# Keys and values of the second attention, projected during routing and kept in device memory

## What is computed

```python
qp = q @ Wq.T
kv = latent_kv @ Wkv_expand.T        # latent_kv is the context: (4, 256, 64)
k, v = jnp.split(kv, 2, axis=-1)
...                                  # 16 heads of 16
scores = jnp.einsum('bhqd,bhkd->bhqk', qh, kh) * inv_sqrt_d
scores = jnp.where(causal, scores, jnp.finfo(scores.dtype).min)
attn = jax.nn.softmax(scores, axis=-1)
out = jnp.einsum('bhqk,bhkd->bhqd', attn, vh)
```

## Time and profile before

| what | value |
|---|---|
| median of 3 runs | 613.92 us (612.71 to 614.38) |
| the profiled execution: its time, its span | 607.06 us, 605.3 us |
| PE busy | 425.7 us (70%), 2738 matmuls |
| DVE busy | 346.5 us (57%) |
| ACT busy | 184.0 us (30%) |
| POOL busy | 146.3 us (24%) |
| mean granted clock of PE | 0.834 of full |

### The profile page before, as it was taken

The page is one execution under the profiler, slowest core; times in us unless marked ns, Lnnn a source line. Parts: engine busy times, 40 slices in busy tenths (PEclk is TensorE's granted clock), DMA queues, the critical chain, the costliest instruction groups (busy, mean ns, idle before and its releaser), DMA issues.

```text
span 605.3 us, 9222 instructions
## 1 busy us (share of the span) xinstructions
PE 425.7 (70%) x2738; PEld 355.7 (59%) x2738; DVE 346.5 (57%) x1050; ACT 184.0 (30%) x377; POOL 146.3 (24%) x154
## 2 busy tenths in 40 slices
PE   5065553302999999997136637899699978999686
PEld 3043342202998889885025425787488856887586
DVE  2978875396344444443367803487547883681554
ACT  3212210100333333343611412525252342517231
POOL 1306675673000000002775370001710000000000
PEclk9976565555999999997557756999779996999899
DMA  7996222266699999993332130000310000000000
GB/s 272 427 410 264 88 96 79 78 238 211 209 301 322 324 312 326 377 396 128 100 91 67 38 104 0 1 2 16 100 44 0 2 0 0 18 2 2 2 17 18
DMA packets 36693, 82.96 MB, mean 137 GB/s; under 512 B 6000, under 2 KB 16048, under 8 KB 34864
## 3 DMA queue, kind: packets, MB, share of 16 engines
q1 hardware_dynamic: 22800, 55.83, 26.3%
q0 software_dynamic: 6144, 16.79, 8.6%
q10 hardware_dynamic: 7712, 9.90, 4.6%
HBM read 50.44 MB, written 31.92 MB: 136 GB/s over the span
## 4 chain that ended last, share of the span: by engine, by line
PE 52%; DVE 15%; issue 12%; ACT 7%; POOL 6%; another core or an unknown queue 4%; DMA 2%; SPq 1%; DVEq 0%; POOLq 0%; ACTq 0%
PE PS L555 11%; PE PS L565 7%; POOL slots_in L432 5%; PE PS L644 4%; PE PS L618 4%; PE PS L542 3%; PE PS L764 2%; PE PS L657 2%; PE PS L712 2%; PE PS L659 2%; PE PS L658 2%; DVE TH L1312 2%; DVE WORK L1049 2%; DVE TOP L1045 2%
## 5 line engine op out<-in xcount | busy, mean ns | idle before, releaser
L442 POOL DMA_INDIRECT GB<-slots_out,IDXG x64 | 68.4, 1069 | 214.9 <-SPq L365 139.7
L555 PE MATMUL PS<-XTE,WR 128*128 128x128 f32 (+2 forms) x512 | 79.7, 299 | 0.0
L432 POOL DMA_INDIRECT slots_in<-XNA,IDX x64 | 64.9, 1014 | 36.8 <-issue 27.6
L555 PEld LDWEIGHTS PS<-XTE,WR 128*128 128x128 f32 x512 | 70.2, 193 | 0.6 <-ACT XTE L854 0.4
L1234 DVE TENSOR_TENSOR HE<-SGE,PS 128x128 f32<-128x128 f32 (+2 forms) x64 | 20.0, 312 | 62.9 <-ACT SGE L863 60.0
L565 PE MATMUL PS<-WR,HE 128*80 128x256 f32 (+2 forms) x198 | 53.6, 381 | 0.3 <-DVE HE L1234 0.3
L657 PE MATMUL PS<-XH,WGH 128*128 128x256 f32 x160 | 49.7, 311 | 0.3 <-DVE XL L1430 0.3
L854 ACT COPY XTE<-PS 128x256 f32<-128x256 f32 (+2 forms) x64 | 26.3, 410 | 74.5 <-PE PS L542 70.6
L644 PE MATMUL PS<-WD,XW 128*128 128x256 f32 x160 | 41.8, 384 | 7.0 <-DVE XW L1319 3.5
L542 PE MATMUL PS<-CF,XE 80*128 80x80 f32 (+2 forms) x198 | 28.3, 256 | 25.7 <-DMA XE<-slots_in 25.7
L658 PE MATMUL PS<-XL,WGH 128*128 128x256 f32 x160 | 45.3, 283 | 0.0
(11 more groups left out here) (226 smaller groups left out, 843.2 us busy)
## 6 DMA issues: line engine op xcount, KB each, us to landing
WR<-in_wexp SPq DMA_DIRECT2D x64, 384.0 KB, 5.0
slots_in<-GB SPq DMA_DIRECT2D x12, 1024.0 KB, 18.7
XE<-slots_in SPq DMA_DIRECT2D x24, 160.0 KB, 4.5
slots_out<-OE ACTq DMA_DIRECT2D x24, 160.0 KB, 4.3
XE<-slots_in SPq DMA_DIRECT2D x29, 128.0 KB, 5.2
slots_out<-OE ACTq DMA_DIRECT2D x29, 128.0 KB, 5.1
WGU<-in_wgu SPq DMA_DIRECT2D x1, 2560.0 KB
XE<-slots_in SPq DMA_DIRECT2D x11, 192.0 KB, 4.0
```

What stands on the lines that cost most here:

```text
L432: pool.indirect_dma_start(out=xs, out_offset=bass.IndirectOffsetOnAxis(ap=IDX[:, t, j:j + 1], axis=0), in_=XNA[:, t, :], in_offset=None, b ...
L442: pool.indirect_dma_start(out=GB[:, t % BT, j, :], out_offset=None, in_=ys, in_offset=bass.IndirectOffsetOnAxis(ap=IDXG[:, t, j:j + 1], ax ...
L555: last = mm(psGE[place % 2][:, a, 0:cap(place)], W13[:, k, a, :], XTE[:, place % 2, k, 0:cap(place)], start=(k == 0), stop=(k == KC - 1))
```

## The change

Keys and values of all four batches are made during routing. The order of work of PE and ACT in that stage is written out by hand: pieces `keys`, `keys_rest` and `spread_keys` (two halves) stand between the steps of the mask, the mix and the router. The low part of the keys is no longer a subtraction of DVE: PE computes the product again and subtracts the high part with a product by a negative identity (NEG) into the same bank, and ACT copies it. ACT copies the spread keys in four parts to a tile KST, and issues two transfers a batch that put KST (1 MB) and VA (512 KB) in device memory. SP loads the three arrays that this needs ahead of x, waits for the last KST before it loads the first slots, and loads KS and VA of batch b+1 back when the last product of turn b with the values (`e_av`) is done. The steps at the ends of the turns and POOL's copies are gone.

The diff, cut to its core:

```diff
+            with ExitStack() as before_experts:
+                def sb_before(name, shape):
+                    return before_experts.enter_context(nc.sbuf_tensor(name, shape, F32R))
+
+                SPREADK = sb_before("SPREADK", [P, 2, UNITS // KC, P])
+                KP = sb_before("KP", [P, 2, KC, N])
+                KST = sb_before("KST", [P, UNITS, N])
...
-        psKc = PS[:, 3, :].rearrange("p (a n) -> p a n", a=2)
+        psKc, psKl = (PS[:, i, :].rearrange("p (a n) -> p a n", a=2) for i in range(2))
+        psKp = PS[:, 0:2, :].rearrange("p b (g n) -> p b g n", g=2)
         psQc = PS[:, 4, :].rearrange("p (a n) -> p a n", a=2)
-        psK = PS[:, 0:4, :].rearrange("p b (g n) -> p (b g) n", g=2)
-        psQ = psK
+        psQ = PS[:, 0:4, :].rearrange("p b (g n) -> p (b g) n", g=2)
...
-        psY = psV = psX2 = psX3 = PS[:, 4, :].rearrange("p (a n) -> p a n", a=2)
+        psV = PS[:, 1, :].rearrange("p (a n) -> p a n", a=2)
+        psY = psX2 = psX3 = PS[:, 4, :].rearrange("p (a n) -> p a n", a=2)
...
+            for dst, src in ((WK1[:, :, :], wk1), (WV1[:, :], wv1), (SPREADB[:, :, :, :], spread)):
+                sp.dma_start(dst, src).then_inc(S["loaded_kv"], 16)
             sp.dma_start(X[:, :, :], x.rearrange("(t p) d -> p t d", p=P)).then_inc(S["loaded_x"], 16)
...
-            for dst, src in ((WQ1[:, :, :, :], wq1), (WK1[:, :, :], wk1), (WV1[:, :], wv1), (WO1[:, :, :], wo1),
-                             (GATE1[:, :, :], gate1), (SPREADB[:, :, :, :], spread), (WGU1[:, :, :, :, :], wgu1), (WD1[:, :, :], wd1)):
+            for dst, src in ((WQ1[:, :, :, :], wq1), (WO1[:, :, :], wo1), (GATE1[:, :, :], gate1), (WGU1[:, :, :, :, :], wgu1), (WD1[:, :, :], wd1)):
...
             sp.wait_ge(S["scattered"], 16 * TT * TOP0)
+            sp.wait_ge(S["ks_kept"], 16 * B)
...
+            def keys_values(b):
+                sp.dma_start(KS[:, :, :].rearrange("p g n -> p (g n)").bitcast(F32), kst[ds(b * P, P), :]).then_inc(S["ks_in"], 16)
+                sp.dma_start(VA[:, :, :, :].rearrange("p t h c -> p (t h c)"), vst[ds(b * P, P), :]).then_inc(S["va_in"], 16)
+
+            def next_keys_values(b):
+
+                sp.wait_ge(S["e_av"], b * HG)
+                keys_values(b)
+
+            sp.wait_ge(S["general_done"], 1)
+            sp.wait_ge(S["oe_copied"], E0)
+            sp.wait_ge(S["va_kept"], 16 * B)
+            keys_values(0)
             maxima_rows(0)
-            with sp.Fori(0, B - 1) as f:
+            next_keys_values(1)
+            with sp.Fori(0, B - 2) as f:
                 maxima_rows(f + 1)
+                next_keys_values(f + 2)
                 store(f)
+            maxima_rows(B - 1)
+            store(B - 2)
...
-            pool.wait_ge(S["pool_set"], 5)
-            nc.gpsimd.tensor_copy(CTB[:, :], CT[:, 0:N]).then_inc(S["e_ctx"], 1)
...
-                if b:
-                    pool.wait_ge(S["e_v"], b)
-                    nc.gpsimd.tensor_copy(CTB[:, :], CT[:, b * N:(b + 1) * N]).then_inc(S["e_ctx"], 1)
...
+            def keys(b):
+                pe.wait_ge(S["qk_copied"], min(b + 2, B))
+                pe.wait_ge(S["sim_copied"], min(b + 2, B))
+                pe.wait_ge(S["ks_set"], b * 4)
+                for m in range(KC):
+                    last = mm(psKc[:, m, :], WK1[:, m, :], CT[:, b * N:(b + 1) * N], start=True, stop=True)
+                last.then_inc(S["k_done"], 1)
+                for t in range(BT):
+                    last = mm(psV[:, t, :], CT[:, b * N + t * P:b * N + (t + 1) * P], WV1[:, :], start=True, stop=True)
+                last.then_inc(S["v_done"], 1)
+
+            def keys_rest(b):
+                pe.wait_ge(S["k_high"], b + 1)
+                pe.wait_ge(S["va_set"], b + 1)
+                for m in range(KC):
+                    mm(psKl[:, m, :], WK1[:, m, :], CT[:, b * N:(b + 1) * N], start=True, stop=False)
+                    last = mm(psKl[:, m, :], NEG[:, :], KP[:, 0, m, :], start=False, stop=True)
+                last.then_inc(S["k_rest"], 1)
+
+            def spread_keys(b, first):
+                pe.wait_ge(S["k_low"], b + 1)
+                for p in range(first, first + 2):
+                    pe.wait_ge(S["ks_set"], b * 4 + max(p - 1, 0))
+                    for g in range(2 * p, 2 * p + 2):
+                        for i in range(2):
+                            last = mm(psKp[:, p % 2, g % 2, :], SPREADK[:, i, g % (UNITS // KC), :], KP[:, i, g // (UNITS // KC), :],
+                                      start=(i == 0), stop=(i == 1))
+                    last.then_inc(S["k_spread"], 1)
+
             scores(0)
             scores(1)
+            pe.wait_ge(S["loaded_kv"], 48)
+            pe.wait_ge(S["spread_set"], 2)
+            keys(0)
+            keys_rest(0)
+            spread_keys(0, 0)
             pe.wait_ge(S["loaded_gate0"], 48)
-            for b in range(B):
-                mix(b)
-                logits(b)
-                ranks(b)
-                if b + 2 < B:
-                    scores(b + 2)
+            mix(0)
+            spread_keys(0, 2)
+            logits(0)
+            ranks(0)
+            pe.wait_ge(S["ks_set"], 4)
+            scores(2)
+            keys(1)
+            mix(1)
+            keys_rest(1)
+            spread_keys(1, 0)
+            logits(1)
+            ranks(1)
+            pe.wait_ge(S["ks_set"], 6)
+            scores(3)
+            pe.wait_ge(S["sim_copied"], 4)
+            spread_keys(1, 2)
+            mix(2)
+            keys(2)
+            logits(2)
+            ranks(2)
+            mix(3)
+            keys_rest(2)
+            spread_keys(2, 0)
+            logits(3)
+            ranks(3)

             for n in range(TT):
                 last = mm(psN, onesb, MB[:, n, :], start=(n == 0), stop=(n == TT - 1))
             for n in range(TT):
                 last = mm(psC, MB[:, n, :], onesb[:, 0:1], start=(n == 0), stop=(n == TT - 1))
             last.then_inc(S["counted"], 1)
+            spread_keys(2, 2)
+            keys(3)
+            keys_rest(3)
             pe.wait_ge(S["order_set"], 1)
             mm(psOrder, numbersb[0:E0, :], OH[0:E0, :], start=True, stop=True)
             mm(psPlace, onesb[0:E0, :], DG[0:E0, :], start=True, stop=True).then_inc(S["order_done"], 1)
+            spread_keys(3, 0)
+            spread_keys(3, 2)
+            pe.wait_ge(S["ks_set"], 4 * B)
...
-            def spread(dst, part, which):
+            def spread(dst, part):

                 for g in range(UNITS):
                     for i in range(2):
-                        last = mm(dst[:, g, :], SPREAD[:, which + i, g % (UNITS // KC), :], part[:, i, g // (UNITS // KC), :],
+                        last = mm(dst[:, g, :], SPREAD[:, i, g % (UNITS // KC), :], part[:, i, g // (UNITS // KC), :],
                                   start=(i == 0), stop=(i == 1))
                 return last
-
-            def keys(b):
-
-                pe.wait_ge(S["e_ctx"], b + 1)
-                for m in range(KC):
-                    last = mm(psKc[:, m, :], WK1[:, m, :], CTB[:, :], start=True, stop=True)
-                last.then_inc(S["e_k"], 1)
-
-            def spread_keys(b):
-                pe.wait_ge(S["e_spread"], 1)
-                pe.wait_ge(S["e_lo_k"], b + 1)
-                spread(psK, KP, 0).then_inc(S["e_k_spread"], 1)
-
-            def values(b):
-                for t in range(BT):
-                    last = mm(psV[:, t, :], CTB[:, t * P:(t + 1) * P], WV1[:, :], start=True, stop=True)
-                last.then_inc(S["e_v"], 1)
...
-                pe.wait_ge(S["e_va"], b + 1)
...
-                pe.wait_ge(S["e_ks"], b + 1)
+                pe.wait_ge(S["e_spread"], 1)
                 pe.wait_ge(S["e_lo_q"], b + 1)
-                spread(psQ, QP, 2).then_inc(S["e_q_spread"], 1)
+                spread(psQ, QP).then_inc(S["e_q_spread"], 1)
...
+                pe.wait_ge(S["ks_in"], b * 16 + 16)
...
+                    if g == 0:
+                        pe.wait_ge(S["va_in"], b * 16 + 16)
...
-                if ahead:
-                    keys(b + 1)
...
-                if ahead:
-                    pe.wait_ge(S["e_x3"], b + 1)
-                    values(b + 1)
-                    spread_keys(b + 1)
-                    pe.wait_ge(S["e_va"], b + 2)
...
-            keys(0)
-            values(0)
-            spread_keys(0)
...
+            def keys(b):
+                act.wait_ge(S["k_done"], b + 1)
+                A.copy(KP[:, 0, :, :], psKc).then_inc(S["k_high"], 1)
+                act.wait_ge(S["v_done"], b + 1)
+                act.wait_ge(S["va_kept"], b * 16)
+                A.copy(VA[:, :, :, 0:HD], psV.rearrange("p t (h c) -> p t h c", h=NH)).then_inc(S["va_set"], 1)
+                act.wait_ge(S["va_set"], b + 1)
+                act.dma_start(vst[b * P:(b + 1) * P, :], VA[:, :, :, :].rearrange("p t h c -> p (t h c)")).then_inc(S["va_kept"], 16)
+
+            def keys_rest(b):
```

(65 more changed lines are left out.)

25 lines of the change are left out of this document (11 added, 14 removed).

## The result

The changed kernel takes 627.39 us (median of 4 runs, 625.3 to 631.01), the kernel before beside it 614.15 (612.71 to 614.41): a ratio of 1.0242, interval 1.0205 to 1.0279. It is slower by 13.2 us where 1.5 were predicted. The profiled execution of after is its longest, 631.01 us with a span of 629.2; that of before (607.06, span 605.3) was faster than all its timed runs. Some executions of a kernel fall into a slower state: every median and ratio from here on is of the others alone, while the traces of f_no_seam_keys, g_order_first, j_early_batch and j2_early_batch are of slower ones.

The account below looks back on a forecast made before the run. It took a chain of waits, half of it PE's, to bound the kernel; 5.0 + 1.0 + 2.0 + 1.5 - 8.0 = +1.5 us on the 613.92 median gave 615.4. The range for 8 in 10 was 608 to 621.

Parts of the forecast that it names:

- Part 3: Routing, batch 0: PE's added keys and spread delay the mix and DVE's statistics; +5.0 us, the largest cost.
- rival 1: Routing: the moved work wakes PE to its high clock level, so the kernel is faster, 607.4 us; chance 0.27.
- Part 4: Routing, batches 1 to 3: added products mostly fit PE's idle time; +1.0 us, bounds 0 and 2.6.
- Part 5: Between ranks and experts: the order's two products come 7.4 us later, mostly covered by idle time; +2.0 us.
- Rival 2: First slots wait for the last key store, landing behind the expert weights: 5 us more, 620.4 us; chance 0.15.
- Part 6: Six MB stored and six loaded back: cost 0, bounds 0 and 2 us for what they do to the gathers.
- Part 1: Ends of turns 1 and 2: without keys and values there they shorten; -8.0 us, bounds 6.5 and 8.4.
- Part 2: End of turn 0: without keys PE idles and may enter the chunks at half clock; +1.5 us, bounds -0.2 and +3.
- Rival 3: Turns: PE waits in the next turn for DVE's maxima or gathered rows, half the gain lost, 619.4 us; chance 0.13.
- DVE's 7 us of idle time: Sign in routing: DVE idle 7 us or more before its first L1086, which starts at 40 to 41.
- the order's 7 us: Sign at the end of routing: the two products of the order come 7 us further behind the ranks.
- the clock after turn 0 under 1.00: Sign after turn 0: PE's granted clock, 1.00 in the kernel before, falls under 1.00.

Follow-up runs that it names:

- f_no_seam_keys: Kernel before with the keys and values of batches 2 and 3 left out, nothing in their place (output wrong in turns 2 and 3): 604.89 us, ratio 0.9924.
- g_order_first: Changed kernel with the two products that give the experts' order put back right behind the counts: 610.72 us, ratio 1.0048.
- j_early_batch: Kernel before with batch 2's keys and values made before the scatters begin, batch 3's behind the order: 583.88 us, ratio 0.9961.
- j2_early_batch: Same version as j_early_batch, run again (kernel before, batch 2's keys ahead of the scatters, batch 3's behind the order): 584.27 us, ratio 0.9960.
- kind B: Groups of runs in which the kernel before takes 585 to 587 us and no kernel has products that reach ACT late.
- kind A: Groups of runs in which the kernel before takes 610 to 614 us and ACT waits 14 to 19 us for late products in turn 0's attention.
- c_kst_moe: Changed kernel with the keys' staging tile put where MOE lies, so the first slots need not wait for the last store: 589.62 us, ratio 1.0073.
- f2: Kernel before without the keys and values of batches 2 and 3, as in f_no_seam_keys, run on kind B: 579.26 us, ratio 0.9873.
- e: Changed kernel unaltered, run again beside the kernel before on kind A: 623.74 us, ratio 1.0256.
- b_few_scatters: Changed kernel with one scatter a tile instead of eight (output wrong), on kind B: 592.37 us, ratio 1.0134.
- k: Kernel before without keys and values of batches 2 and 3, plus ten unread PE products in the ends of turns 1 and 2: 578.13 us, ratio 0.9838.
- j3: Same version as j_early_batch, run a third time, on kind A: 605.76 us, ratio 0.9928.
- d2_filler_again: Kernel before with ten unread PE products added behind the mix of batches 1, 2 and 3, on kind A: 622.07 us, ratio 1.0156.

## Why the prediction was wrong

The sign was right, the time was not: 13.2 us against 1.5. By its own steps:

- **Part 3 (batch 0, +5.0): right.** The statistics come 5.63 us later, the places 4.6. PE took the low durations as forecast (keys 2.04, values 1.91, the first half of the spread 2.08 us), so rival 1 failed where it was to decide.
- **Part 4 (batches 1 to 3, +1.0, bounds 0 and 2.6): right on kind B, wrong on kind A.** In c_kst_moe the places of the four batches are later than in f2 by 2.9, 2.6, 2.5, 2.5 us: batches 1 to 3 add nothing. In after they add 7.5, in e 4.5. The cover was there on kind B; what failed on kind A is the step that prices PE's products by their rows wherever they stand. On this kind of chip products beside the scatters are late, and turn 0 of before, where ACT lost 15 us in the attention, had shown it: I had these waits in the trace and did not ask what would set them off elsewhere.
- **Part 5 (order, +2.0, bounds 0 and 2.3): the step that failed.** The lateness of the two products was sized well (the order came 9.9 us after the places of batch 3, before 1.5: 8.3 more, forecast 7.4). Wrong was the path. The part prices the wait through DVE and the tokens' weights, and the first expert's product on DVE still had 5.73 us of idle time. It says of the weights that they "still land ahead of the first expert", which they did. But the path that ended last goes through their request: SP asks for them 28.9 us later and issues the slots only behind them (request 8.2 us later), and 3 MB are on the way when the last scatters (6.99 us to landing instead of 2.41 in c_kst_moe) and the slots (7.8 instead of 2.7) want the DMA engines. Moving the order back gave 13.0 us, where the part had 2.0.
- **Rival 2 (slots wait for the last store, +5): it didn't happen in the profiled execution.** The store was issued at 156.00, where 133.4 on the old clock was forecast, and still the slots came behind SP's own issues, with no wait for it. Where it was the last to come, in b_few_scatters, it took 6.48 us and not twice 7.9.
- **Part 6 (transfers, 0 to 2): wrong** for the reason of Part 5. The loads for the turns did cost nothing: PE has no wait for KS or VA in the trace of after. The bounds that the prediction adds up leave this part's 2 us out.
- **Part 1 (-8.0): right in mechanism, its size not settled.** Two measurements of the ceiling: 4.6 us on kind A (2.7 to 6.6), 7.5 on kind B by the ratio (3.5 to 11.3). In single traces the two stretches are shorter by 5.7 us in after, 1.2 in f, 5.9 in f2, 8.0 in k, 9.0 in j3. At the seams themselves after takes 8.09 us in turn 1 (465.42 to 473.51) and 9.13 in turn 2 (528.54 to 537.67), f2 7.85 and 7.79, where 7.79 was forecast for both. What is missing in turn 2 is the clock behind the norm: 4.30 us at a mean of 0.68 in after (533.37 to 537.67), 2.95 us at 1.00 in f2 (484.59 to 487.54). The end of turn 3 loses 1.4 us in the same way. I had allowed for the clock in turn 0 (Part 2) and almost not here.
- **Part 2 (+1.5, bounds -0.2 and +3): the clock after turn 0 is 0.69 where it was 1.00**, and the stretch to the next addition is 3.5 us longer in after, 1.4 in e. But that clock is 0.65 in f2 and 0.58 in f too, which keep their keys there, and 0.79 in d2_filler_again, whose turns are those of before: I can't put it down to the change.
- **Rival 3 (gain given back):** in part, beside a lower clock and not by waits for DVE.

```profile
407.00:415.00 8.00, 8.00 (x41) 7.71 (x42) 4.01 (x22) 4.05 (x10) 0.00 (x0) 0.69 0.00 0
```

Of the signs named in the prediction, DVE's 7 us of idle time (8.10), the order's 7 us and the clock after turn 0 under 1.00 hold; the last batch's first scatter was to come at 126 to 127 and came at 132.55, and the first HE was to be without its 5 us of idle time and had 5.73: the slots had become what is late.

## What to carry to other kernels

A step that only sets off a large load is on the path through what the load collides with, and through the engine that issues it: ask not only when it lands but what small transfers it meets on the way, and what stands behind it in the order of its engine. Put new PE work where the transfers of the same time are few, and before adding it look in the trace for products that ended by PE's records but whose reader waited; where there are such waits, more products cost more than their rows. When work is taken away from PE, look at the granted clock behind it before the whole gain is counted: here the same steps took 4.40 us at 0.66 and 2.97 us at 1.00.

## What the runs showed of the hardware

The same kernel takes 610 to 614 us in four comparisons and 585 to 587 in three others, and late products appear in the first four alone. There, ten idle products in each of three batches beside scatters cost 1.6%, a whole batch of keys ahead of them nothing. In the trace of after SP's register steps behind the loads of the order, too, take 0.44 us at the median instead of 0.15. What the engines share there was not found. The Trainium skill (NOTIFIC — the notification-queue block, 7.1 Overflow: three behaviours, one of which stalls the engine) says that the path which writes the engines' trace records can hold back those that produce them; no run here tests whether that is it.
